# Attention probabilities weighted for two key tiles per visit of TensorE, with four buffers instead of two

## The chip, the core and the metric

The kernel runs on one core of one Trainium2 chip. The metric is the device time of one execution in microseconds; a kernel's time is the median of several.

## The reference

x has two rows of 1024 tokens with 128 channels, in float32. Four layers are added to it one after the other: a gated recurrence with an MLP, a mixture of low-rank experts, an attention, and the experts again. The change is in the attention:

```python
attn = jax.nn.softmax(jnp.einsum('bhqd,bhkd->bhqk', q, k) * scale, axis=-1)
...
attn = attn + rel_bias
out = jnp.einsum('bhqk,bhkd->bhqd', attn, v)
```

There are 16 heads of 8 channels, so per row and head a matrix of 1024 x 1024 scores, its softmax, and the values weighted with it.

## The kernel before

The kernel is written engine by engine: each has its own program, and they meet at counting semaphores. No scheduler changes the order; what stands in a program is done in that order, and a wait holds up all that is behind it on its engine.

The attention works on 8 groups, each four heads of one row of the input. A group has 16 **steps**: two halves of 512 queries (q) times eight tiles of 128 keys (t). In step s:

- TensorE makes four **scores** (`scores`, L1402), one head each: 128 keys x 512 queries into one of three PSUM banks. A score waits until the third exponential before it is done.
- ScalarE takes the exponential of each (`step`, L731) into a buffer of probabilities, `probs[s % 2]`. Before a step it waits (`pv_done`) until the weighing that read this buffer is done.
- TensorE **weighs** the values with the probabilities of the step before (`weigh`, L1416): four float32 matmuls of 128 keys x 32 columns, one per head, each on its own 32 columns of the array, all added up in the bank `pv_bank` over eight steps. The profile records each as two passes, so a weighing is 8 records. Once per half, ScalarE copies the bank out (`take_pv`, L721).

Beside the scores of one group TensorE and VectorE work on the **ring**: 36 items per group that go through two slots of two PSUM banks each. 32 items are products for the maxima of the next groups (`max_item`, L1339, two matmuls of 512 columns), which VectorE reduces (L1028). The others are the turn of the 32 maxima (L1345, which VectorE splits in three parts, L1033 to L1039), the bias product (L1353), its turn (L1359) and the turn of the output (L1366). An item is filled when the item two before it has been emptied (`ring_emptied`). `beside` deals the items to the steps: two for each, three for every fourth. In a step TensorE does, in this order: score 0, item, score 1, score 2, weighing, item, score 3, and a third item if there is one.

A round begins at step 2 (`FIRST`) of a group and ends with step 1 of the next. Six rounds run in a loop of two passes over three rounds; then comes the round that prepares the last group, with no items for a group after it, and the last group's own steps, among which the first pieces of the last expert layer stand. The weighing of a group's last step is made in step 0 of the next group, or after the steps for the last group.

```python
RING = NEXT_MAXES[:4] + [("bias", 0, 0), NEXT_MAXES[4], ("bias_turn", 0, 0)] + NEXT_MAXES[5:] + AFTER_NEXT + [("out", 0, 0)]
...
    return banks[:, 2 * (n % 2):2 * (n % 2) + 2, :]
...
    share = RING[j * len(RING) // STEPS:(j + 1) * len(RING) // STEPS]
```

## Time and profile before

| what | value |
|---|---|
| median of 3 runs | 742.9 us (740.99 to 742.91) |
| the profiled execution, from first to last instruction | 738.4 us |
| TensorE busy (matmul) | 666.5 us, 90% |
| VectorE busy | 533.7 us, 72% |
| ScalarE busy | 381.2 us, 52% |
| mean granted clock of TensorE | 0.961 |

The span is that of one profiled execution; for it no time is recorded apart from the span, and the runs' median lies 4.5 us above it. A busy time is the time in which at least one instruction of the engine ran. Where engines hand work to each other all the time, the share alone does not say which of them sets the pace; that is read from what each waits for. The attention's steps lie between 256 and 664 us.

### The profile page before, as it was taken

The page shows a single profiled execution, that of the slowest core. Times are in us where ns is not written, and L with a number is a line of the kernel's source. Part 1 is how long each engine was busy: PE and PEld are TensorE (multiplying, and loading weights), DVE is VectorE, ACT ScalarE, POOL GpSimd, SP SyncE. Part 2 cuts the span into 40 slices and gives each one's busy share as a digit, 9 for nine tenths or more (in the row PEclk, how much of TensorE's full clock was granted, in tenths as well). Part 3 has the DMA queues.
Part 4 walks back from the last instruction along what each step waited for, and adds up shares of the span by engine and source line. Part 5 has one row for each costly group of instructions (what it writes and reads, how often), then busy time and mean ns, then how long its engine had stood idle before and what let it go on. Part 6 is the DMA issues. An engine that isn't in the chain of part 4 may idle for free.

```text
span 738.4 us, 10515 instructions
## 1 busy us (share of the span) xinstructions
PE 666.5 (90%) x3192; PEld 254.5 (34%) x3192; DVE 533.7 (72%) x956; ACT 381.2 (52%) x687; POOL 104.9 (14%) x100
## 2 busy tenths in 40 slices
PE   3988898999777699999999899999999998988997
PEld 1434344444343222332322232332322322324443
DVE  5379788746699868868878768868788688308744
ACT  2745133333203057767767657766667677882231
POOL 5910110001044411020020020020100202002000
PEclk9998899999969789999999999999999999999999
DMA  8000000000313102012012020030120000000000
GB/s 253 5 1 0 1 0 1 1 0 0 112 67 122 58 28 95 2 41 83 4 56 66 17 83 28 18 99 9 32 91 3 2 0 2 2 1 0 1 28 28
DMA packets 21413, 26.59 MB, mean 36 GB/s; under 512 B 3312, under 2 KB 12016, under 8 KB 21360
## 3 DMA queue, kind: packets, MB, share of 16 engines
q1 hardware_dynamic: 20496, 25.39, 10.8%
q8 instruction: 29, 0.48, 0.3%
q0 software_dynamic: 144, 0.52, 0.2%
q14 instruction: 24, 0.20, 0.1%
q10 hardware_dynamic: 720, 0.00, 0.1%
HBM read 21.52 MB, written 4.19 MB: 35 GB/s over the span
## 4 chain that ended last, share of the span: by engine, by line
PE 69%; DVE 19%; ACT 4%; issue 2%; DMA 2%; DVEq 1%; POOL 1%; SPq 1%; POOLq 0%; ACTq 0%
PE banks L1416 17%; PE banks L1339 15%; PE banks L1402 14%; PE banks L1154 6%; DVE negmax L1028 6%; PE banks L1224 4%; PE banks L1265 3%; PE banks L1353 2%; PE banks L1215 2%; PE banks L1161 2%; DVE arena L886 1%; ACT arena L731 1%; DVE arena L936 1%; DVE stats L783 1%; PE banks L1366 1%
## 5 line engine op out<-in xcount | busy, mean ns | idle before, releaser
L1028 DVE TENSOR_REDUCE negmax<-banks 128x1 f32<-128x1024 f32 x256 | 300.8, 1217 | 68.6 <-PE banks L1339 67.4
L731 ACT ACTIVATE arena<-banks 128x512 f32<-128x512 f32 x512 | 271.7, 601 | 144.1 <-PE banks L1402 140.6
L1339 PE MATMUL banks<-arena 72*128 72x512 bf16 x512 | 161.3, 400 | 23.6 <-DVE negmax L1028 19.7
L1402 PE MATMUL banks<-arena 75*128 75x512 bf16 x512 | 160.2, 384 | 6.7 <-ACT arena L731 3.1
L1416 PE MATMUL banks<-arena 128*32 128x512 f32 x1024 | 138.1, 612 | 0.7 <-ACT arena L731 0.7
L1339 PEld LDWEIGHTS banks<-arena 72*128 72x128 bf16 x512 | 37.8, 100 | 163.0 <-DVE negmax L1028 77.0
L1402 PEld LDWEIGHTS banks<-arena 75*128 75x128 bf16 x512 | 48.6, 98 | 95.7 <-ACT arena L731 48.0
L495 POOL TENSOR_TENSOR rstd<-veps,neghalf 128x4 f32<-128x4 f32 (+1 forms) x24 | 27.1, 1129 | 247.3 <-DVE veps L802 192.1
L1224 PE MATMUL banks<-arena,bT 128*128 128x512 f32 x128 | 60.1, 593 | 1.6 <-ACT arena L585 1.6
L585 ACT ACTIVATE arena<-banks 128x512 f32<-128x512 f32 (+1 forms) x56 | 32.2, 595 | 53.1 <-PE banks L1154 22.7
L886 DVE TENSOR_SCALAR arena<-banks,bi 128x512 f32<-128x512 f32 x32 | 23.8, 745 | 34.7 <-PE banks L1224 34.7
L562 POOL TENSOR_TENSOR pause<-neghalf 128x8 f32<-128x8 f32 x7 | 1.4, 199 | 309.9 <-PE banks L1353 309.9
L1224 PEld LDWEIGHTS banks<-arena,bT 128*128 128x128 f32 x128 | 24.2, 190 | 32.2 <-issue 29.9
L1416 PEld LDWEIGHTS banks<-arena 128*32 128x32 f32 x1024 | 20.3, 108 | 39.3 <-issue 33.2
L1215 PE MATMUL banks<-hT,wiT 128*128 128x512 f32 x64 | 32.9, 615 | 0.0
L1161 PE MATMUL banks<-ident,nt 128*128 128x128 f32 x80 | 13.7, 313 | 20.4 <-DVE nt L812 11.9
L546 POOL TENSOR_TENSOR arena<-arena,t_last 128x2048 f32<-128x2048 f32 x8 | 28.8, 3599 | 0.0
L585 ACT ACTIVATE hT<-banks 128x512 f32<-128x512 f32 x12 | 6.8, 596 | 31.8 <-PE banks L1161 31.8
L1265 PE MATMUL banks<-arena,woT 128*128 128x512 f32 x48 | 22.1, 597 | 0.3
L585 ACT ACTIVATE x<-banks,bi 128x512 f32<-128x512 f32 x16 | 11.0, 687 | 20.3 <-PE banks L1224 20.3
L783 DVE BATCH_NORM_STATS2 stats<-x 128x6 f32<-128x128 f32 x80 | 17.4, 280 | 5.4 <-DMA x<-in_x 4.5
L585 ACT ACTIVATE oT<-banks,bo 128x512 f32<-128x512 f32 x8 | 5.5, 687 | 30.4 <-PE banks L1265 30.4
(128 smaller groups left out, 614.1 us busy)
## 6 DMA issues: line engine op xcount, KB each, us to landing
arena<-qk_scratch SPq DMA_DIRECT2D x192, 48.0 KB
arena<-in_tab SPq DMA_DIRECT2D x8, 1024.0 KB, 6.8
qk_scratch<-arena SPq DMA_DIRECT2D x8, 384.0 KB, 2.8
out<-x SPq DMA_DIRECT2D x4, 256.0 KB, 2.3
x<-in_x SPq DMA_DIRECT2D x1, 512.0 KB, 4.5
x<-in_x POOLq DMA_DIRECT2D x1, 512.0 KB, 7.7
arena<-nm_part SPq DMA_DIRECT2D x24, 8.0 KB, 1.9
w_aT<-in_w_aT SPq DMA_DIRECT2D x1, 256.0 KB, 6.5
```

Source lines behind the costliest of these rows:

```text
L546: pool.tensor_tensor(varying, bias_raw[:, :, ::-1], t_last[:, bass.ds(G * GH, GH)].unsqueeze(2).broadcast_to([P, GH, BIASW]), ALU.subtract ...
L585: act.activation(dst, banks[:, BANK[name], :], func, **kw).then_inc(signal or act_emptied, 1)
L731: act.activation(probs[s % 2][:, h, :], score_bank(g, n), ACT.Exp, scale=SCALE).then_inc(exp_done, 1)
L886: dve.tensor_scalar(h1[:, c % 2, :], bank(name), bi[:, c:c + 1], 0.0, ALU.add, ALU.max).then_inc(dve_emptied, 1)
L1028: return dve.tensor_reduce(negmax[:, buf, k:k + 1], slot.rearrange("p a b -> p (a b)"), axis=AXX, op=ALU.max, negate=True)
L1154: last = pe.matmul(banks[:, BANK[name], :], lhsT, rhs, start=i == 0, stop=i == len(terms) - 1)
L1215: pe.matmul(banks[:, BANK[name], :], chunk(wiT, c), half(hT[:, b], h), start=True, stop=False, skip_group_check=True)
L1224: pe.matmul(banks[:, BANK[name], :], chunk(bT, c), half(moe[b][4][:, k, :], h), start=False, stop=k == 1, skip_group_check=True).then_inc( ...
L1265: last = pe.matmul(banks[:, BANK[name], :], woT[:, c, :], moe[b][2][h][:, c, :], start=c == 0, stop=c == FC - 1)
L1339: last = pe.matmul(slot[:, half_, :], qs[0:STACK, buf, h, t * P:(t + 1) * P], ks[0:STACK, buf, h, half_ * HALF:(half_ + 1) * HALF], start= ...
L1402: pe.matmul(score_bank(g, n), ks[0:DEPTH, g % BUFS, h, t * P:(t + 1) * P], qs[0:DEPTH, g % BUFS, h, q * HALF:(q + 1) * HALF], start=True, ...
L1416: last = pe.matmul(pv_bank[32 * h:32 * h + VW, :], vpg[:, g % BUFS, t, h, :], probs[s % 2][:, h, :], start=t == 0, stop=t == NT - 1)
```

## The change

`probs` gets two more buffers, in tiles that lie idle during the attention (x0 and oT, each 128 x 2048 float32 by the view taken of it). ScalarE writes step s into `probs[s % 4]`. TensorE no longer weighs in every step: in an even step s it weighs the steps s-2 and s-1 one right after the other, in the place where the single weighing stood, and in an odd step not at all. Step 0 of a group takes the last two of the group before. ScalarE copies the weighed bank out in step 1 and step 9, behind the first exponential, where before it did so in step 0 and step 8, behind the third. Its waits on `pv_done` follow.

```diff
--- before.py
+++ after.py
@@ -314,6 +314,8 @@
         qk_part = [m.bitcast(BF16).rearrange("p (w n t) -> p w n t", w=2, n=NPART) for m in (words_0, words_1)]
 
         probs = [m.rearrange("p w t -> p (w t)").rearrange("p (h t) -> p h t", h=GH) for m in qk_rest]
+
+        probs += [m[:].rearrange(f"p {axes} -> p ({axes})").rearrange("p (h t) -> p h t", h=GH) for m, axes in ((x0, "b t c"), (oT, "b t"))]
         varying = words_1[:, 0:GH * BIASW].rearrange("p (h c) -> p h c", h=GH)
         qs = q_words.bitcast(BF16).rearrange("p (n h t) -> p n h t", n=BUFS, h=GH)
 
@@ -722,16 +724,16 @@
 
             def step(G, g, s):
 
-                if s >= 2 or not (isinstance(G, int) and G == 0):
-
-                    act.wait_ge(pv_done, at(G, pv_done, s - 1))
+                if s >= len(probs) or (s < FIRST and not (isinstance(G, int) and G == 0)):
+
+                    act.wait_ge(pv_done, at(G, pv_done, 0 if s == 1 else s - len(probs) + 1))
                 for h in range(GH):
                     n = s * GH + h
                     act.wait_ge(scores_filled, at(G, scores_filled, n + 1))
-                    act.activation(probs[s % 2][:, h, :], score_bank(g, n), ACT.Exp, scale=SCALE).then_inc(exp_done, 1)
-                    if h == GH - 2 and s == 0 and not (isinstance(G, int) and G == 0):
+                    act.activation(probs[s % len(probs)][:, h, :], score_bank(g, n), ACT.Exp, scale=SCALE).then_inc(exp_done, 1)
+                    if h == 0 and s == 1 and not (isinstance(G, int) and G == 0):
                         take_pv(G - 1, 1)
-                    if h == GH - 2 and s == NT:
+                    if h == 0 and s == NT + 1:
 
                         act.wait_ge(ring_filled, at(G, ring_filled, 0))
                         take_pv(G, 0)
@@ -1413,9 +1415,18 @@
 
                         pe.wait_ge(pv_out, at(G, pv_out, q))
                 for h in range(GH):
-                    last = pe.matmul(pv_bank[32 * h:32 * h + VW, :], vpg[:, g % BUFS, t, h, :], probs[s % 2][:, h, :],
+                    last = pe.matmul(pv_bank[32 * h:32 * h + VW, :], vpg[:, g % BUFS, t, h, :], probs[s % len(probs)][:, h, :],
                                      start=t == 0, stop=t == NT - 1)
                 last.then_inc(pv_done, 1)
+
+            def weigh_two(G, g, s):
+
+                if s:
+                    weigh(G, g, s - 2)
+                    weigh(G, g, s - 1)
+                elif not (isinstance(G, int) and G == 0):
+                    weigh(G - 1, g - 1, STEPS - 2)
+                    weigh(G - 1, g - 1, STEPS - 1)
 
             def step(G, g, s, fill_item, ring):
 
@@ -1424,10 +1435,8 @@
                     fill_item(ring[0])
                 scores(G, g, s, 1)
                 scores(G, g, s, 2)
-                if s:
-                    weigh(G, g, s - 1)
-                elif not (isinstance(G, int) and G == 0):
-                    weigh(G - 1, g - 1, STEPS - 1)
+                if s % 2 == 0:
+                    weigh_two(G, g, s)
                 if len(ring) > 1:
                     fill_item(ring[1])
                 scores(G, g, s, 3)
@@ -1501,7 +1510,7 @@
                     logits(1, 0)
                 if s == X_STEP:
                     turn_products(1, 0)
-            weigh(G, G, STEPS - 1)
+            weigh_two(G + 1, G + 1, 0)
             for c in range(FC):
                 base(1, 0, c)
                 if c == 0:
```

On TensorE, here are two steps of the straight part behind the loop, in the round that prepares the last group (steps 6 and 7 of a group, with two items each), from one weighing to the next but one. L1416 is the weighing, L1402 a score, L1339 the product for a maximum. Before:

```order
L1416 MATMUL banks<-arena 32x512 x4
L1339 MATMUL banks<-arena 128x512 x2
L1402 MATMUL banks<-arena 128x512 x2
L1339 MATMUL banks<-arena 128x512 x2
L1402 MATMUL banks<-arena 128x512 x2
L1416 MATMUL banks<-arena 32x512 x4
L1339 MATMUL banks<-arena 128x512 x2
L1402 MATMUL banks<-arena 128x512 x2
L1339 MATMUL banks<-arena 128x512 x2
L1402 MATMUL banks<-arena 128x512 x2
L1416 MATMUL banks<-arena 32x512 x4
```

In the changed kernel the same stretch reads (L1418 is the weighing, L1404 the score, L1341 the product; x and oT are the new buffers):

```order
L1418 MATMUL banks<-arena 32x512 x8
L1341 MATMUL banks<-arena 128x512 x2
L1404 MATMUL banks<-arena 128x512 x2
L1341 MATMUL banks<-arena 128x512 x2
L1404 MATMUL banks<-arena 128x512 x2
L1341 MATMUL banks<-arena 128x512 x2
L1404 MATMUL banks<-arena 128x512 x2
L1341 MATMUL banks<-arena 128x512 x2
L1404 MATMUL banks<-arena 128x512 x2
L1418 MATMUL banks<-x,arena 32x512 x4
L1418 MATMUL banks<-oT,arena 32x512 x4
```

Between two visits there are now four products and eight scores in a row, and each visit has eight matmuls instead of four.

The second place is on TensorE too, in the same round behind the last product for a maximum, where steps have no items left; L1345 is the turn of the maxima. Before:

```order
L1345 MATMUL banks<-ident,negmax 32x128
L1402 MATMUL banks<-arena 128x512 x2
L1416 MATMUL banks<-arena 32x512 x4
L1402 MATMUL banks<-arena 128x512 x4
L1416 MATMUL banks<-arena 32x512 x4
L1402 MATMUL banks<-arena 128x512 x4
L1416 MATMUL banks<-arena 32x512 x4
```

And in the changed kernel:

```order
L1347 MATMUL banks<-ident,negmax 32x128
L1404 MATMUL banks<-arena 128x512 x6
L1418 MATMUL banks<-arena 32x512 x8
L1404 MATMUL banks<-arena 128x512 x8
L1418 MATMUL banks<-x,arena 32x512 x4
L1418 MATMUL banks<-oT,arena 32x512 x4
```

Here eight scores stand between two visits, where four stood before.

## Rows read from the trace of the kernel before

**Rows 1.** Groups of instructions in one round, 323.2 to 373.9 us

```profile
L1028 DVE TENSOR_REDUCE negmax<-banks 128x1 f32<-128x1024 f32 x33 | 38.8, 1217 | 8.3 <-PE banks L1339 8.2 <-issue 0.2
L731 ACT ACTIVATE arena<-banks 128x512 f32<-128x512 f32 x65 | 34.6, 601 | 16.2 <-PE banks L1402 15.7
...
L1339 PE MATMUL banks<-arena 72*128 72x512 bf16 x64 | 19.3, 382 | 0.9 <-DVE negmax L1028 0.9
L1416 PE MATMUL banks<-arena 128*32 128x512 f32 x128 | 17.1, 605 | 0.0
```


**Rows 2.** The chain that ended last (start us, us, what)

```profile
272.51 2.29 PE banks L1353 x32
...
323.24 2.29 PE banks L1353 x32
...
350.86 0.99 PE banks L1416 x8
...
356.68 0.99 PE banks L1416 x8
```


**Rows 3.** Timeline (start us, us, engine, line, what), three steps

```profile
328.84 1.06 PE L1416 MATMUL banks<-arena 128*32 128x512 f32 x8
...
330.48 3.48 DVE L1028 TENSOR_REDUCE negmax<-banks 128x1 f32<-128x1024 f32 x3 [1.42 <-PE banks L1339]
...
331.76 0.60 PE L1339 MATMUL banks<-arena 72*128 72x512 bf16 x2 [0.45 <-DVE negmax L1028]
...
332.20 0.60 PE L1402 MATMUL banks<-arena 75*128 75x512 bf16 x2
...
332.73 1.07 PE L1416 MATMUL banks<-arena 128*32 128x512 f32 x8
...
333.73 0.61 PE L1339 MATMUL banks<-arena 72*128 72x512 bf16 x2
...
334.37 2.36 DVE L1028 TENSOR_REDUCE negmax<-banks 128x1 f32<-128x1024 f32 x2 [0.41 <-PE banks L1339]
...
335.56 1.06 PE L1416 MATMUL banks<-arena 128*32 128x512 f32 x8
```


**Rows 4.** Timeline, TensorE's weight loads at a bias product

```profile
323.16 0.16 PEld L1353 LDWEIGHTS banks<-arena 128*32 128x32 f32 x8 [0.42 <-issue]
...
323.62 0.13 PEld L1353 LDWEIGHTS banks<-arena 128*32 128x32 f32 x4 [0.30 <-issue]
324.05 0.13 PEld L1353 LDWEIGHTS banks<-arena 128*32 128x32 f32 x4 [0.30 <-issue]
```


**Rows 5.** Timeline, a step without products

```profile
614.30 1.06 PE L1416 MATMUL banks<-arena 128*32 128x512 f32 x8
...
615.30 0.82 PE L1402 MATMUL banks<-arena 75*128 75x512 bf16 x3
...
615.73 2.06 ACT L731 ACTIVATE arena<-banks 128x512 f32<-128x512 f32 x4 [0.33 <-PE banks L1402]
...
616.38 0.39 PE L1402 MATMUL banks<-arena 75*128 75x512 bf16 x1 [0.26 <-ACT arena L731]
...
616.70 1.07 PE L1416 MATMUL banks<-arena 128*32 128x512 f32 x8
```


**Rows 6.** Timeline, VectorE around the split of the maxima

```profile
354.94 0.28 DVE L1033 CAST nm_part<-banks 32x128 bf16<-32x128 f32 x1 [0.16 <-PE banks L1345]
...
355.30 0.28 DVE L1035 TENSOR_TENSOR nm_rest<-banks,nm_part 32x128 f32<-32x128 f32 x1
...
356.17 3.47 DVE L1028 TENSOR_REDUCE negmax<-banks 128x1 f32<-128x1024 f32 x3
```


**Rows 7.** Windows (from:to, us, busy us and count per engine, granted clock)

```profile
418.00:422.00 4.00, 1.71 (x11) 0.86 (x9) 2.20 (x6) 0.99 (x3) 0.00 (x0) 1.00 0.12 33
422.00:430.00 8.00, 8.00 (x45) 2.09 (x48) 4.59 (x4) 4.22 (x8) 0.00 (x0) 0.79 0.18 59
640.00:664.00 24.00, 21.03 (x124) 5.32 (x124) 5.11 (x19) 20.42 (x42) 0.00 (x0) 1.00 0.00 1
```


## The prediction

> **What bounds the kernel now.** I began with the page's part on costly groups, narrowed to one round of the attention [rows 1]. A round is one group of four heads: 50.73 us from one bias product to the next [rows 2]. In it VectorE spends 38.8 us in 33 maxima and is idle 8.3 us before them, waiting for TensorE's products; ScalarE spends 34.6 us in exponentials and is idle 16.2 us, again only for TensorE (L1402). No row has ScalarE waiting for a weighing, which is what a buffer of probabilities comes free with. So the two further buffers by themselves buy nothing; what counts is the order on TensorE.
>
> Then the timeline, step by step [rows 3]. A plain step (four scores, two products for maxima, one weighing) goes from the weighing at 332.73 to that at 335.56: 2.83 us. Matmuls of 512 columns follow each other at 0.217 us, a product for a maximum (two of them) takes 0.435, and the weighing takes 1.00 from its start to the next matmul. The two scores ahead of it start at 332.20 and would be through at 332.64, so 0.09 us more go in before it. Sum: 4 x 0.217 + 2 x 0.435 + 1.09 = 2.83. TensorE paces this step. One step in four has a third product and takes 3.89 us (328.84 to 332.73), where its own work is 3.26: the rest it stands still ahead of the product at 331.76 (idle 0.45 in the row), until VectorE's first reduce has released a slot.
>
> That gives VectorE's three constants, all from [rows 3]. Its reduce starts 0.64 us after the product's first matmul (333.73 to 334.37). Reduces follow each other at 1.13 us (three in 3.48, the last 1.22 long). TensorE enters the slot again 1.28 us after the reduce's start (330.48 to 331.76). There are two slots. Check: from the end of a weighing the next product is at 0, its reduce at 0.64, its slot free at 1.92; then one product, two scores, the entry and the weighing, 0.435 + 0.434 + 0.09 + 1.00 = 1.96: 3.88, against 3.89 measured.
>
> **The change, part by part.** The visits go from one per step to one of two weighings in every even step; 128 visits (eight groups of 16 steps) become 64, with the same matmuls in all.
>
> *What a merged visit saves.* The bias product is the same kind of matmul, four groups in a row without a switch [rows 4]. Its first group starts at 323.16, the second pass at 323.62, the next group at 324.05. So a group of 512 columns takes 0.88 us when another follows, and the 0.12 on top in a single visit is paid on leaving. A double visit is then D = 0.88 + 1.00 = 1.88 us, with the same 0.09 ahead. Against two singles (2.18) it saves 0.21 us; 64 of them, if TensorE paced everything, 13.4 us. The Trainium skill, page TensorEngine Tiling (Array Packing), "Key Properties", says that changing the tiling mode drains TensorE. The trace agrees (0.09 and 0.12 us), and by that rule alone the change is right. The same page, "PSUM Bottleneck", warns that emptying PSUM may become the bound.
>
> *What it costs.* TensorE now feeds VectorE nothing for 1.88 us at a time, and VectorE can hold at most two filled slots. I walk one pair (light step, then the heavy step with the visit) from the end of a visit:
> - product A starts at 0, its reduce at 0.64, its slot is free at 1.92
> - product B, the light step's first, is filled well before VectorE comes to it; its reduce is at 0.64 + 1.13 = 1.77, its slot free at 1.77 + 1.28 = 3.05
> - product C, the light step's second, goes into A's slot at 1.92; its reduce is at 2.90
> - product D, the heavy step's first, needs B's slot. With nothing to wait for TensorE would be there at 2.61 (six scores and three products); it starts at 3.05, and two scores, the visit and everything behind are queued after it
> - 0.435 + 0.434 + 0.09 = 0.96 later the visit starts, at 4.01, and ends at 5.89.
>
> Two plain steps took 5.67: **+0.22**. With a third product in the light step one more reduce lies in the way: 5.89 + 1.13 = 7.02, against 3.89 + 2.83 = 6.72: **+0.30**. D's reduce starts at 2.90 + 1.13 = 4.03 and is over at 5.25, so VectorE idles from there to 5.89 + 0.64, 1.3 us a pair; that is where the saved switches go. ScalarE does not matter here: a pair's eight exponentials take some 3.9 us at 0.49 each [rows 5].
>
> *The pairs of one round* (eight):
> - three plain pairs: 3 x 0.22 = 0.66
> - two with a third product: 2 x 0.30 = 0.60
> - the pair with the turn of the maxima. Its split holds VectorE for 1.23 us (354.94 to 356.17) and gives its slot back at 355.58 [rows 6]. The turn's slot is free at 1.92; the split runs behind product B's reduce, from 2.90 to 4.13. C now waits for B's slot (3.05), D starts at 3.70 (the turn's slot is free at 3.54), the visit at 4.66, its end is 6.54. Today the two steps take 356.68 - 350.86 = 5.82 [rows 2]: +0.72. Dear, because today the step's wait hides the split
> - the pair with the bias product (2.29 us, TensorE's own) starts it at 3.05 rather than at once and comes to +0.1. The one after it, whose turn of the bias costs VectorE 0.28, to -0.1: zero together.
>
> Sum 1.98 us a round. Six full rounds: 11.9. The seventh has its products up to the turn: +0.7. Its last steps and the last group run without products.
>
> *Steps without products.* Today one takes 2.40 us (614.30 to 616.70), set by ScalarE: with three score banks the step's third score comes 0.65 after the previous step's last exponential starts (615.73 to 616.38), the visit 0.32 behind it, its end 1.00 later, and the fourth score's exponential 0.43 after that (615.30 to 615.73) [rows 5]. With a double visit: 0.65 + 0.32 + 1.88 + 0.43 = 3.28 to that exponential, and four more at 0.49 (four in 2.06, the last 0.6 long) until the light step's last: 5.24, against 4.80: +0.4. Of ten such pairs about five are bare (+2.0); three hold transposes or logits, which fill the wait (about +0.5 together); at the end the last exponentials and one joint visit replace two (about -0.5). I take +2.0.
>
> Total 11.9 + 0.7 + 2.0 = +14.6 us: span 738.4 to 753.0. The median 742.9 lies 4.5 above the profiled span, and I leave that as it is: **757.5 us**.
>
> The take-over of the weighed bank by ScalarE moves one step later, behind a score that exists anyway. The next visit is over 5 us off, so I cost it at nothing; uncovered it is 0.6 us (one activation), 16 times. That ScalarE passes over no visit wait is in [rows 1]. The new wait for weighings ahead of a step's exponentials asks for a visit that TensorE makes before it issues that step's scores.
>
> **Bounds.** The least D is four passes at 0.43 with nothing for switching, 1.72 [rows 4]: 0.16 less in 63 pairs, 747. Product waits that come 0.1 later each (semaphores, register updates) in the 53 pairs with products: 762.
>
> **Rivals.**
> 1. *Faster: TensorE paces all the pairs.* Then 13.4 us go: 729.5. For it: today TensorE's matmul groups show almost no idle before them (0.9 us at L1339 [rows 1]). Against it: the pair's length by VectorE's chain is 4.01 + D, so it turns only at D under 1.66, less than four passes. Or the release at 1.28 would have to fall by over 0.2. Chance 0.07.
> 2. *Same: the losses come only where a third product or the turn stands* (2 x 0.30 + 0.72 a round), and the other five pairs gain 0.21 each: +0.3 a round, +2, and as much back from the pairs at the end: about 743. Chance 0.05.
> 3. *Slower still: the clock falls.* At 418 to 422 TensorE is busy 1.71 of 4.00 us and the granted clock in the next 8 us is 0.79, part at 1.2 GHz instead of 2.4 [rows 7]: 0.21 x 8 = 1.7 us. One such dip a round more: 757.5 + 13 = 771. Against it: from 640 to 664 TensorE is busy 21.0 of 24 us, in gaps like those I expect, and the clock stays 1.00. The Trainium skill, page TensorE: Matmul & The Clock Gate, "A second HAM failure mode: psum-queue depth-cycling", tells of short idle times between matmul groups that make the clock swing; no row here shows that. Chance 0.05.
>
> The forecast (starved VectorE, 747 to 764) has 0.83. That the change would not do what it says I leave out: the order of the built program shows the double visits.
>
> **Numbers.** A measurement here can tell 0.3%, 2.2 us. Range 747 to 766: the bounds, with a little above for smaller clock losses; 0.07 + 0.05 + part of 0.05 and some of the spread lie outside. Faster 0.07 (rival 1), same 0.04, slower 0.89 (rival 2 mostly counts as same).
>
> **What the trace after would show.** Double visits of 1.88 us in 16 records; visits of even steps 5.9 and 7.0 us apart; the heavy step's first product waiting for a reduce; VectorE idle some 1.3 us before the reduce behind each visit; a round of 52.7 us; pairs without products 5.2 us apart. I am wrong if the visits come 5.4 us apart and VectorE's idle time there is under 1 us (rival 1), if D is not 1.88, or if the clock column shows new dips.

## The result: 3.9% slower, more than forecast

| | before | changed |
|---|---|---|
| median | 741.94 us (740.50 to 742.91) | 769.60 us (764.44 to 772.35) |
| ratio of the times, 95% interval | | 1.039 [1.034, 1.044] |
| span of the profiled execution | 738.4 us | 762.7 us |

Forecast were 757.5 us and a range up to 766. The side was right, the size was not. Medians here are over all executions of a kernel, while ratios leave out executions over 1.5% above that kernel's fastest, so a ratio can differ from the quotient of the medians beside it.

From the page of the changed kernel: the engines' busy times, VectorE's maxima and TensorE's products for them (busy us, mean ns of one, idle us before them and what ended it):

```profile
span 762.7 us, 10501 instructions
...
PE 677.1 (89%) x3192; PEld 262.1 (34%) x3192; DVE 531.3 (70%) x956; ACT 375.4 (49%) x687; POOL 105.2 (14%) x100
...
L1030 DVE TENSOR_REDUCE negmax<-banks 128x1 f32<-128x1024 f32 x256 | 298.3, 1217 | 88.3 <-PE banks L1341 86.9
L1341 PE MATMUL banks<-arena 72*128 72x512 bf16 x512 | 162.7, 403 | 30.8 <-DVE negmax L1030 24.8
```

The same two lines of the kernel before:

```profile
L1028 DVE TENSOR_REDUCE negmax<-banks 128x1 f32<-128x1024 f32 x256 | 300.8, 1217 | 68.6 <-PE banks L1339 67.4
...
L1339 PE MATMUL banks<-arena 72*128 72x512 bf16 x512 | 161.3, 400 | 23.6 <-DVE negmax L1028 19.7
```

VectorE does the same 256 maxima, but waits 86.9 us for products instead of 67.4, and TensorE waits 24.8 us for VectorE instead of 19.7. Both waits grew, as two engines do that hand work to each other through too few slots; the walk below shows that it is so. A pair of steps without a third product, in the timeline (start us, us, engine, line, what):

```profile
345.51 1.93 PE L1418 MATMUL banks<-arena 128*32 128x512 f32 x16
...
347.37 0.60 PE L1341 MATMUL banks<-arena 72*128 72x512 bf16 x2
...
348.01 4.62 DVE L1030 TENSOR_REDUCE negmax<-banks 128x1 f32<-128x1024 f32 x4 [1.27 <-PE banks L1341]
...
348.24 0.59 PE L1341 MATMUL banks<-arena 72*128 72x512 bf16 x2
...
349.29 0.60 PE L1341 MATMUL banks<-arena 72*128 72x512 bf16 x2
...
350.42 0.60 PE L1341 MATMUL banks<-arena 72*128 72x512 bf16 x2
...
350.86 0.60 PE L1404 MATMUL banks<-arena 75*128 75x512 bf16 x2
...
351.39 1.06 PE L1418 MATMUL banks<-x,arena 128*32 128x512 f32 x8
```

Read it against [rows 3]. The visit is one run of 16 records, and the next product starts 1.86 us after it (345.51 to 347.37; forecast 1.88). VectorE has waited 1.27 us (forecast 1.3) and reduces four slots in a row. The heavy step's first product stands at 350.42, 3.05 behind the first product, to the hundredth as the walk had it; only then come two scores and the next visit. From visit to visit: 351.39 - 345.51 = 5.88 us, forecast 5.89. The pair with the turn of the maxima, from its first product on:

```profile
353.25 0.60 PE L1341 MATMUL banks<-arena 72*128 72x512 bf16 x2
...
355.17 0.28 PE L1347 MATMUL banks<-ident,negmax 128*32 128x128 f32 x1
...
356.16 0.27 DVE L1035 CAST nm_part<-banks 32x128 bf16<-32x128 f32 x1
...
356.30 0.61 PE L1341 MATMUL banks<-arena 72*128 72x512 bf16 x2 [0.63 <-DVE negmax L1030]
...
356.96 0.59 PE L1341 MATMUL banks<-arena 72*128 72x512 bf16 x2
...
357.92 1.93 PE L1418 MATMUL banks<-arena 128*32 128x512 f32 x16
```

Product C waits for B's slot (idle 0.63 in its row) and starts 3.05 us behind the first product (353.25 to 356.30), as forecast. The visit comes 357.92 - 351.39 = 6.53 us after the one before (forecast 6.54). Pairs with a third product take 7.01 and 7.09 (forecast 7.02).

Where the 24.3 us of span went. The cuts are the starts of the first score, of the bias products (as in [rows 2]) and of the last pass of the last weighing:

| stretch | before | changed | difference | forecast |
|---|---|---|---|---|
| start to first score | 256.2 | 252.9 | -3.3 | 0 |
| to the first bias product | 16.3 | 17.5 | +1.2 | 0 |
| five rounds | 50.73 each | 52.69 each | +9.8 | +9.9 |
| the round across the loop's jump | 54.59 | 58.45 | +3.9 | +2.0 |
| 7th bias product to 8th | 43.2 | 47.4 | +4.2 | +2.7 with the next |
| 8th bias product to the last weighing's last pass | 39.4 | 47.9 | +8.5 | |
| the rest | 75.0 | 75.05 | 0 | 0 |

So the rounds came out as computed, +1.96 against +1.98. The excess stands at the end, where steps have no products, and in the round across the jump (there TensorE's clock is at half for 6.8 us instead of 3.4). Windows of the changed kernel's end (from:to, us, busy us and count of PE, PEld, DVE, ACT, POOL, granted clock, two DMA columns):

```profile
640.00:650.00 10.00, 9.61 (x81) 3.23 (x74) 1.28 (x4) 5.89 (x12) 0.00 (x0) 1.00 0.00 0
660.10:663.50 3.40, 3.40 (x17) 0.60 (x16) 1.88 (x6) 1.17 (x3) 0.00 (x0) 0.50 0.00 0
666.90:670.30 3.40, 3.37 (x15) 0.69 (x17) 0.00 (x0) 1.71 (x4) 0.00 (x0) 0.50 0.00 0
680.50:684.00 3.50, 3.50 (x17) 0.59 (x16) 0.00 (x0) 1.21 (x3) 0.00 (x0) 0.51 0.02 5
```

Three stretches at 0.50, that is 1.2 GHz instead of 2.4, and a fourth at 625.9; the ten us from 640 are at full clock. The kernel before had none from 425.4 us to its end. A fifth, at 704.4, lies behind the attention, where the time did not change (75.05 us against 75.02). The other new thing is a wait that I had costed at nothing:

```profile
636.65 0.60 ACT L723 ACTIVATE arena<-banks 128x512 f32<-128x512 f32 x1
...
637.40 1.06 PE L1368 MATMUL banks<-ident,arena 128*128 128x128 f32 x8 [1.54 <-ACT arena L723]
```

The turn of the output stands 1.54 us still until ScalarE has taken the weighed bank over.

### The profile page after: what moved, and what is told of

It is laid out like the page before. It is cut to its first block, busy times and chain, and to the rows that moved or that the text cites. A ratio compares the mean times of both kernels' runs of the same rounds, so it can differ in the third digit from the quotient of the medians.

```text
span 762.7 us, 10501 instructions
## 1 busy us (share of the span) xinstructions
PE 677.1 (89%) x3192; PEld 262.1 (34%) x3192; DVE 531.3 (70%) x956; ACT 375.4 (49%) x687; POOL 105.2 (14%) x100
## 4 chain that ended last, share of the span: by engine, by line
PE 54%; DVE 26%; issue 9%; ACT 5%; DVEq 2%; DMA 2%; POOL 1%; SPq 1%; POOLq 0%; ACTq 0%
PE banks L1418 17%; DVE negmax L1030 14%; PE banks L1341 10%; PE banks L1404 6%; PE banks L1156 6%; PE banks L1226 4%; PE banks L1355 2%; PE banks L1267 2%; PE banks L1217 2%; PE banks L1163 2%; DVE arena L888 1%; ACT oT L733 1%; DVE arena L938 1%; PE banks L1368 1%; DVE stats L785 1%
## 5 line engine op out<-in xcount | busy, mean ns | idle before, releaser
L1030 DVE TENSOR_REDUCE negmax<-banks 128x1 f32<-128x1024 f32 x256 | 298.3, 1217 | 88.3 <-PE banks L1341 86.9
L1341 PE MATMUL banks<-arena 72*128 72x512 bf16 x512 | 162.7, 403 | 30.8 <-DVE negmax L1030 24.8
L733 ACT ACTIVATE arena<-banks 128x512 f32<-128x512 f32 x256 | 138.7, 612 | 94.5 <-PE banks L1404 94.3
L1404 PE MATMUL banks<-arena 75*128 75x512 bf16 x512 | 164.1, 389 | 10.0 <-issue 2.7
L733 ACT ACTIVATE x<-banks 128x512 f32<-128x512 f32 x128 | 72.7, 600 | 84.9 <-PE banks L1404 84.0
L1341 PEld LDWEIGHTS banks<-arena 72*128 72x128 bf16 x512 | 37.3, 100 | 147.1 <-DVE negmax L1030 110.0
L1404 PEld LDWEIGHTS banks<-arena 75*128 75x128 bf16 x512 | 49.2, 98 | 98.7 <-ACT arena L733 19.3
L1418 PE MATMUL banks<-arena 128*32 128x512 f32 x512 | 69.0, 661 | 0.0
L733 ACT ACTIVATE oT<-banks 128x512 f32<-128x512 f32 x128 | 66.0, 612 | 0.0
L1418 PE MATMUL banks<-x,arena 128*32 128x512 f32 x256 | 35.0, 619 | 0.0
L1418 PE MATMUL banks<-oT,arena 128*32 128x512 f32 x256 | 34.1, 605 | 0.1
L1418 PEld LDWEIGHTS banks<-arena 128*32 128x32 f32 x512 | 14.3, 117 | 36.9 <-issue 29.5
```

Source lines behind the costliest of these rows:

```text
L733: act.activation(probs[s % len(probs)][:, h, :], score_bank(g, n), ACT.Exp, scale=SCALE).then_inc(exp_done, 1)
L1030: return dve.tensor_reduce(negmax[:, buf, k:k + 1], slot.rearrange("p a b -> p (a b)"), axis=AXX, op=ALU.max, negate=True)
L1341: last = pe.matmul(slot[:, half_, :], qs[0:STACK, buf, h, t * P:(t + 1) * P], ks[0:STACK, buf, h, half_ * HALF:(half_ + 1) * HALF], start= ...
L1404: pe.matmul(score_bank(g, n), ks[0:DEPTH, g % BUFS, h, t * P:(t + 1) * P], qs[0:DEPTH, g % BUFS, h, q * HALF:(q + 1) * HALF], start=True, ...
L1418: last = pe.matmul(pv_bank[32 * h:32 * h + VW, :], vpg[:, g % BUFS, t, h, :], probs[s % len(probs)][:, h, :], start=t == 0, stop=t == NT - 1)
```

## Experiments

The theory after the result had three parts: (V) in the rounds VectorE's two slots set the pair, as forecast; (E) at the end the double visit holds ScalarE's chain up, and the later take-over holds the turn of the output up; (C) the longer waits of TensorE lower its clock more often. Rivals: the four buffers themselves cost something; the take-over is the cause; the clock alone is.

**Buffers alone.** The kernel before with the four buffers and their waits, one weighing a step.

```diff
+        probs += [m[:].rearrange(f"p {axes} -> p ({axes})").rearrange("p (h t) -> p h t", h=GH) for m, axes in ((x0, "b t c"), (oT, "b t"))]
...
+                    act.wait_ge(pv_done, at(G, pv_done, 0 if s == 1 else s - len(probs) + 1))
...
+                    act.activation(probs[s % len(probs)][:, h, :], score_bank(g, n), ACT.Exp, scale=SCALE).then_inc(exp_done, 1)
```

> The kernel before with four buffers of probabilities and still one weighing per step. Theory (what costs time is the order on TensorE, not the buffers): same time as before, 741.9 us within 2, rounds of 50.7 us. Rival (the buffers in x0 and oT cost something, or the later release helps): more than 745 or less than 740 us.

740.04 us against 739.93; 0.999 [0.996, 1.003]; a round 50.71 us. Within 0.4%, the buffers neither cost nor bring anything. The loss comes with the order on TensorE and the later take-over, a loss of clock that they bring included.

**Singles at the end, doubles in the rounds.**

```diff
@@ -1437,3 +1437,6 @@
                 scores(G, g, s, 2)
-                if s % 2 == 0:
+                last = isinstance(G, int) and (G == GROUPS - 1 or (G == GROUPS - 2 and s > 12))
+                if last:
+                    weigh(G if s else G - 1, g if s else g - 1, (s - 1) % STEPS)
+                elif s % 2 == 0:
                     weigh_two(G, g, s)
@@ -1512,3 +1515,3 @@
                     turn_products(1, 0)
-            weigh_two(G + 1, G + 1, 0)
+            weigh(G, G, STEPS - 1)
             for c in range(FC):
```

> The changed kernel, but from step 13 of the seventh group on one weighing per step again. Theory (about half of the loss sits in the steps without products: ScalarE starved, a new wait for the take-over, clock dips that these gaps bring): rounds stay at 52.7 us, the stretch from the seventh bias product to the last weighing falls from 95.3 us to some 83.5, no dips there, 752 to 756 us in all. Rival (the dips come by chance or from the rounds): the clock dips stay and the time is above 762 us.

760.85 us, 1.027 [1.022, 1.033]. The rounds stay at 52.69. The stretch from the seventh bias product to the last weighing takes 46.0 + 39.9 = 85.9 us against 95.3, and no part of it is at half clock. The same windows of both kernels, the changed one first:

```profile
600.00:650.00 50.00, 44.59 (x266) 13.38 (x265) 34.40 (x87) 32.00 (x62) 4.12 (x4) 0.97 0.00 1
650.00:688.00 38.00, 33.38 (x172) 10.14 (x170) 7.13 (x29) 25.46 (x52) 0.00 (x0) 0.87 0.00 1
```

```profile
600.00:650.00 50.00, 45.49 (x284) 13.64 (x282) 36.43 (x90) 33.64 (x65) 7.41 (x5) 1.00 0.01 1
650.00:688.00 38.00, 34.34 (x200) 11.97 (x200) 9.29 (x37) 28.94 (x58) 0.00 (x0) 1.00 0.00 1
```

With single visits TensorE is busy 45.49 and 34.34 us there instead of 44.59 and 33.38, and the clock is 1.00 in both. The time came out over the 752 to 756 expected. The end is 2.4 us longer than the 83.5 expected. In the profile the edit takes 9.4 us off the end, but the first score comes at 257.4 us instead of 252.9, in code that the edit does not touch, so the spans differ by 4.7 only (758.0 and 762.7). Over all profiled executions with whole reduces, of the kernel before and of the changed ones, the first score comes at 250.9 to 258.1 us; single spans compare kernels no closer than that. Parts E and C share the end; this edit does not separate them.

**Doubles at the end, singles in the rounds.**

```diff
@@ -1437,3 +1437,7 @@
                 scores(G, g, s, 2)
-                if s % 2 == 0:
+                last = isinstance(G, int) and (G == GROUPS - 1 or (G == GROUPS - 2 and s > 14))
+                if not last:
+                    if s or not (isinstance(G, int) and G == 0):
+                        weigh(G if s else G - 1, g if s else g - 1, (s - 1) % STEPS)
+                elif s % 2 == 0:
                     weigh_two(G, g, s)
```

> The reverse: one weighing per step up to step 14 of the seventh group, pairs only behind it. Theory: rounds of 50.7 us as before, the stretch from the seventh bias product to the last weighing at 93 to 95 us with clock dips, 752 to 757 us in all. Rival (the end costs what I predicted, 2 us): 744 us.

The six executions lie far apart: their median is 762.13 us, and the ratio, 1.021 [1.013, 1.029], rests on three of them (751.51, 753.54 and 761.18 us). The profiled one took 764.73, with some 91 us at half clock against 74 in the changed kernel's. In it the end is 46.6 + 46.5 us, as expected, with half-clock stretches at 633, 667 and 681. The rounds are 52.02, not the 50.7 expected:

```profile
346.35 1.06 PE L1418 MATMUL banks<-oT,arena 128*32 128x512 f32 x8
...
349.18 0.60 ACT L723 ACTIVATE arena<-banks 128x512 f32<-128x512 f32 x1
...
349.84 1.07 PE L1418 MATMUL banks<-arena 128*32 128x512 f32 x8 [0.58 <-ACT arena L723]
```

With take-overs in steps 1 and 9 a single visit waits for the bank twice a round, 3.49 us from visit to visit instead of 2.83, which makes up the 1.29 us. So the later take-over costs nothing only where visits are a pair apart. Some 8 us of this kernel's loss are of that kind and not the end's, so its time says less about the end than was meant.

**The take-over where it was.**

```diff
@@ -733,5 +733,5 @@
                     act.activation(probs[s % len(probs)][:, h, :], score_bank(g, n), ACT.Exp, scale=SCALE).then_inc(exp_done, 1)
-                    if h == 0 and s == 1 and not (isinstance(G, int) and G == 0):
+                    if h == GH - 2 and s == 0 and not (isinstance(G, int) and G == 0):
                         take_pv(G - 1, 1)
-                    if h == 0 and s == NT + 1:
+                    if h == GH - 2 and s == NT:
```

> The changed kernel with ScalarE's copy of the weighed bank back in steps 0 and 8, behind the third exponential, as before the change. Theory (the later copy only matters where no products stand between it and the turn of the output, once, in the last round): rounds 0.1 us shorter, the wait of 1.5 us ahead of the last round's turn of the output gone, 1 to 3 us faster than the changed kernel. Rival (the later copy hides ScalarE's wait for the visit in every round): rounds longer by 0.3 us or more each, slower by 2 us or more.

766.72 us, 1.032 [1.026, 1.038] over four of six executions; rounds 52.69 as in the changed kernel, 7th to 8th bias product 46.07 instead of 47.37: the 1.3 us of the wait at the turn of the output. The rest of the end takes 44.5 us instead of 47.9, with one half-clock stretch instead of three. In the total that is within the spread: the changed kernel beside it has 1.038 [1.034, 1.043].

**The heavy step's first product behind its third score.**

```diff
@@ -1433,3 +1433,3 @@
                 scores(G, g, s, 0)
-                if len(ring) > 0:
+                if len(ring) > 0 and s % 2:
                     fill_item(ring[0])
@@ -1437,2 +1437,4 @@
                 scores(G, g, s, 2)
+                if len(ring) > 0 and s % 2 == 0:
+                    fill_item(ring[0])
                 if s % 2 == 0:
```

> The changed kernel, in which an even step makes its first product behind the third score, right before the double visit, so that VectorE has more left to do when TensorE turns away. Theory (VectorE starved through two slots sets the pair): plain pairs 5.63 instead of 5.88 us, those with a third product 6.59 instead of 7.01, rounds of some 50.4 us; the end as in the changed kernel; 750 to 757 us. Rival (TensorE's own work or the weighing sets the pair): rounds stay at 52.7 us and the time at 765 to 770.

764.65 us, 1.034 [1.029, 1.039]; a round 52.48, expected 50.4: a miss. Third-product pairs came down to 6.58 as expected, but plain pairs went up to 6.08:

```profile
348.74 0.10 PEld L1404 LDWEIGHTS banks<-arena 75*128 75x128 bf16 x1 [0.40 <-ACT oT L733]
...
348.97 0.60 PE L1341 MATMUL banks<-arena 72*128 72x512 bf16 x2
...
349.50 1.07 PE L1418 MATMUL banks<-x,arena 128*32 128x512 f32 x8
349.61 1.23 DVE L1030 TENSOR_REDUCE negmax<-banks 128x1 f32<-128x1024 f32 x1 [0.20 <-PE banks L1341]
```

The wait is now at a score: its weight load (the first row) stands 0.40 us until ScalarE (L733) is done. With three score banks the heavy step's third score can go 3.47 us after the visit's end. From there 0.22 + 0.435 (the product now behind it) + 0.09 + 1.88 make 6.09 us. VectorE waits a mere 0.20. So a second chain, ScalarE's, lies just under VectorE's: without the product in it, 3.47 + 0.22 + 0.09 + 1.88 = 5.66 us a pair.

**VectorE made faster, in both kernels.** Before, and the same edit on the changed kernel:

```diff
@@ -730,3 +730,3 @@
                     act.wait_ge(scores_filled, at(G, scores_filled, n + 1))
-                    act.activation(probs[s % 2][:, h, :], score_bank(g, n), ACT.Exp, scale=SCALE).then_inc(exp_done, 1)
+                    act.activation(probs[s % 2][:, h, :], score_bank(g, n), ACT.Exp, scale=SCALE / 8).then_inc(exp_done, 1)
                     if h == GH - 2 and s == 0 and not (isinstance(G, int) and G == 0):
@@ -1027,3 +1027,3 @@
             def max_item(slot, buf, k):
-                return dve.tensor_reduce(negmax[:, buf, k:k + 1], slot.rearrange("p a b -> p (a b)"), axis=AXX, op=ALU.max, negate=True)
+                return dve.tensor_reduce(negmax[:, buf, k:k + 1], slot[:, 0, :], axis=AXX, op=ALU.max, negate=True)
```

> The kernel before with reduces over 512 of the 1024 columns (maxima over half the keys, and a smaller exponent so that nothing overflows; the computation is changed), so that VectorE is out of the way. Every theory: plain steps stay at 2.83 us, steps with a third product lose VectorE's wait, 3.26 instead of 3.89; rounds of some 48.3 us.

716.8 us in one execution; rounds 49.38, plain steps 2.83 as they were, third-product steps 3.36 instead of 3.89. The round was expected at 48.3: the third-product steps kept 0.10 us over 3.26, the step with the turn of the output came down to 3.71 only, and the one with the bias product (4.79) not at all.

> The same two edits in the changed kernel (maxima over half the keys, a smaller exponent). Theory of two chains (VectorE's through the two slots gives 5.88 us a plain pair, and behind it ScalarE's through the three score banks gives 3.47 + 0.22 + 0.09 + 1.88 = 5.66): plain pairs 5.66, pairs with a third product 5.88, so that even with a fast VectorE merging gives nothing on a plain pair. Rival (VectorE alone eats the gain): plain pairs at TensorE's own 5.45.

725.8 us in one execution; rounds 48.72. Plain pairs, visits in the timeline:

```profile
331.80 1.92 PE L1418 MATMUL banks<-arena 128*32 128x512 f32 x16
...
337.45 1.06 PE L1418 MATMUL banks<-x,arena 128*32 128x512 f32 x8
```

5.65 us, where ScalarE's chain gives 5.66. Third-product pairs 6.14 (expected 5.88). The rounds of the changed kernel are now the shorter by 0.66 us, where with whole reduces they are the longer by 1.96: that bears V out, VectorE's slots turn the merging's gain in the rounds into a loss. The total is still 9 us longer than its counterpart's, all of it outside these rounds: the end takes 7.1 us more, the round across the jump 3.6, the start 1.6, and the five rounds 3.3 less.

**ScalarE made faster as well.**

```diff
@@ -732,3 +732,3 @@
                     act.wait_ge(scores_filled, at(G, scores_filled, n + 1))
-                    act.activation(probs[s % len(probs)][:, h, :], score_bank(g, n), ACT.Exp, scale=SCALE).then_inc(exp_done, 1)
+                    act.activation(probs[s % len(probs)][:, h, 0:HALF // 2], score_bank(g, n)[:, 0:HALF // 2], ACT.Exp, scale=SCALE / 8).then_inc(exp_done, 1)
                     if h == 0 and s == 1 and not (isinstance(G, int) and G == 0):
@@ -1029,3 +1029,3 @@
             def max_item(slot, buf, k):
-                return dve.tensor_reduce(negmax[:, buf, k:k + 1], slot.rearrange("p a b -> p (a b)"), axis=AXX, op=ALU.max, negate=True)
+                return dve.tensor_reduce(negmax[:, buf, k:k + 1], slot[:, 0, :], axis=AXX, op=ALU.max, negate=True)
```

> The changed kernel with reduces over half the columns and exponentials over 256 of the 512 queries (the other half of the probabilities is left as it was, and the exponent is smaller; the computation is changed): VectorE and ScalarE are both out of the way. Theory: plain pairs at TensorE's own 8 x 0.217 + 4 x 0.435 + 0.09 + 1.88 = 5.45 us, with a third product 5.88. Rival (a merged visit costs TensorE something that I don't see): 5.6 or more.

711.8 us in one execution; rounds 47.6. The visits:

```profile
332.87 1.92 PE L1418 MATMUL banks<-arena 128*32 128x512 f32 x16
...
338.30 1.07 PE L1418 MATMUL banks<-x,arena 128*32 128x512 f32 x8
```

5.43 us. TensorE's own work is 8 x 0.217 + 4 x 0.435 + 0.09 + 1.88 = 5.45: only now does it pace the pair. The three bounds of a plain pair in the changed order are 5.88 (VectorE's slots), 5.66 (score banks), 5.45 (TensorE).

**Three repairs together**: singles at the end, the take-over as it was, the heavy step's product behind the third score.

> Three edits in the changed kernel together: one weighing per step from step 13 of the seventh group on, the even step's first product behind the third score, and the copy of the weighed bank in steps 0 and 8. Theory: the sum of the single effects: rounds of 52.3 us, the end within 3 us of the kernel before, 2 to 2.6% slower than before. Rival (together they free the gain of the merged visits): within 0.5% of the kernel before.

754.32 us, 1.019 [1.014, 1.024]; rounds 52.48. The end takes 83.2 us, against 82.7 in the kernel before. It is the best version with double visits, and still slower than before.

**The waits at the end filled** with scores computed twice (same operands, same bank), so that TensorE is not idle.

```diff
@@ -1403,4 +1403,7 @@
                 t, q = s % NT, s // NT
-                pe.matmul(score_bank(g, n), ks[0:DEPTH, g % BUFS, h, t * P:(t + 1) * P], qs[0:DEPTH, g % BUFS, h, q * HALF:(q + 1) * HALF],
-                          start=True, stop=True).then_inc(scores_filled, 1)
+                idle = isinstance(G, int) and (G == GROUPS - 1 or (G == GROUPS - 2 and s > 13)) and h in ((2, 3) if s % 2 else (0, 1))
+                for _ in range(1 + idle):
+                    last = pe.matmul(score_bank(g, n), ks[0:DEPTH, g % BUFS, h, t * P:(t + 1) * P], qs[0:DEPTH, g % BUFS, h, q * HALF:(q + 1) * HALF],
+                                     start=True, stop=True)
+                last.then_inc(scores_filled, 1)
```

> The changed kernel; in the steps without products, where TensorE stands and waits for ScalarE, each score that follows such a wait is computed twice into its bank (the second result is the same), so that TensorE is busy instead of idle. It is more work for nothing. Theory (the gaps let the granted clock fall, and that costs some 8 us at the end): no dips between the turn of the last maxima and the last weighing, the stretch from the seventh bias product to the last weighing at 87 to 89 us instead of 95.3, and the kernel 5 to 8 us faster than the changed one. Rival (the dips come by chance, or cost nothing): dips stay, the same time as the changed kernel or up to 2 us slower.

767.14 us, 1.037 [1.032, 1.042], beside the changed kernel again:

> The changed kernel once more, beside the next three on the same chip. Every theory: 3.4 to 4.4% over the kernel before, rounds of 52.7 us.

769.27 us, 1.038 [1.034, 1.043]. In the profiles the end of the filled kernel takes 91.8 us with one half-clock stretch, that of the changed kernel beside it 97.1 with five. But 87 to 89 us with none were expected, and a kernel 5 to 8 us faster; the medians differ by 2.1 us and the intervals overlap.

**Waits filled in the rounds too.** Two duplicates at a heavy step's first score and one at a light step's third, in place of that condition:

```diff
+                    if late:
+                        idle = h in ((2, 3) if s % 2 else (0, 1))
+                    else:
+                        idle = (h == 2) if s % 2 else 2 * (h == 0)
```

> The changed kernel; scores are computed twice (the second result is the same), and where TensorE stands waiting longest three times, in the rounds too, so that it has hardly an idle moment. Theory (its gaps in the rounds and at the end let the granted clock fall, which costs some 10 us in most executions): mean granted clock 0.953 or more instead of 0.944, rounds no longer than 53.2 us, 3 us or more faster than the changed kernel. Rival (the clock falls for another reason): clock at 0.94 to 0.95, the same time or slower.

774.13 us, 1.047 [1.041, 1.053]. The mean clock is 0.957, where the changed kernel's 16 executions have 0.946 (other chips, so this is the weaker comparison), but rounds were 54.47 us (expected 53.2 at most): plain pairs take 6.08 instead of 5.88, since the duplicates push the heavy step's first product back. With one duplicate in place of two:

```diff
+                        idle = (h == 2) if s % 2 else (h == 0)
```

> Like the kernel with scores computed twice everywhere, but never three times, which there made each pair 0.2 us longer (the first product of the even step then came at 3.26 instead of 3.05 us). Now the repeats fit into the waits. Theory (the gaps cost clock, and the clock costs time): plain pairs at 5.88 as in the changed kernel, mean granted clock 0.953 or more, 5 us or more faster than the changed kernel on this chip. Rival (what raised the clock there were the longer rounds, or the clock's falls cost nothing here): clock below 0.950, or the time within 3 us of the changed kernel.

> The changed kernel beside the next two on the same chip: 3.4 to 4.4% over the kernel before, mean granted clock near 0.944.

765.74 us, 1.035 [1.031, 1.039], beside 766.43, 1.036 [1.031, 1.040] for the changed kernel. The clock part held, mean 0.956 against 0.948. Windows in the rounds, of the changed kernel in this third profile, then of the filled one:

```profile
343.00:346.80 3.80, 3.17 (x14) 0.97 (x13) 3.80 (x4) 3.62 (x7) 0.00 (x0) 1.00 0.32 125
346.80:350.20 3.40, 3.40 (x16) 0.77 (x18) 1.90 (x2) 1.11 (x3) 0.00 (x0) 0.50 0.02 5
350.20:360.00 9.80, 9.04 (x51) 2.71 (x44) 7.14 (x7) 6.43 (x13) 0.00 (x0) 1.00 0.00 1
...
568.70:572.10 3.40, 3.40 (x17) 0.54 (x16) 1.18 (x2) 0.92 (x2) 0.00 (x0) 0.50 0.00 0
```

```profile
346.80:350.20 3.40, 3.40 (x24) 1.01 (x22) 2.14 (x2) 1.66 (x4) 0.00 (x0) 1.00 0.00 0
500.00:560.00 60.00, 58.43 (x359) 19.62 (x356) 45.05 (x47) 38.59 (x74) 4.09 (x3) 1.00 0.19 57
```

At 346.8 and 568.7 the changed kernel is at 0.50, and each such stretch makes its round 54.3 to 54.4 instead of 52.69, +1.6 to +1.7; the filled kernel, busy 58.43 of 60 us, keeps 1.00. But its rounds are 53.23: plain pairs still take 5.88, and the pairs with the turn of the maxima and of the output 0.2 us more each, where duplicates delay products. The gain of 5 us expected was not there. The longer rounds account for some 3 us of it; that the clock gave as much is not shown by itself.

**The idea turned on the kernel before**: in steps 2, 6, 10 and 14, behind which a third product is waited for, the first product goes behind the third score.

```diff
@@ -1422,3 +1422,4 @@
                 scores(G, g, s, 0)
-                if len(ring) > 0:
+                late = s % 4 == 2
+                if len(ring) > 0 and not late:
                     fill_item(ring[0])
@@ -1426,2 +1427,4 @@
                 scores(G, g, s, 2)
+                if len(ring) > 0 and late:
+                    fill_item(ring[0])
                 if s:
```

> The kernel before (one weighing per step), where in the step after one with a third product the first product comes behind the third score instead of behind the first. The same chain of constants says: it may start at 1.92 us behind the weighing, TensorE does three scores meanwhile, the pair's first step takes 3.45 instead of 3.89 us, rounds 1.3 to 1.7 us shorter, 730 us or 1.1 to 1.5% faster than before, clock no lower. Rival (another chain, ScalarE's, takes over as it did in the changed kernel): rounds within 0.3 us of 50.73 and the same time.

735.58 us against 739.23; **0.995 [0.991, 0.999]** over ten of twelve executions. Over all, the means are 736.6 (12) and 739.8 (17), 0.4% apart. So it is probably a little faster than the kernel before, near the limit of what a comparison tells here, and not by the 1.1 to 1.5% expected. The timeline of one such step:

```profile
330.71 5.82 DVE L1028 TENSOR_REDUCE negmax<-banks 128x1 f32<-128x1024 f32 x5 [1.42 <-PE banks L1339]
...
331.17 0.81 PE L1402 MATMUL banks<-arena 75*128 75x512 bf16 x3
...
332.00 0.61 PE L1339 MATMUL banks<-arena 72*128 72x512 bf16 x2
...
332.53 1.07 PE L1416 MATMUL banks<-arena 128*32 128x512 f32 x8
...
333.53 0.61 PE L1339 MATMUL banks<-arena 72*128 72x512 bf16 x2
```

Three scores run where TensorE stood still in [rows 3], and the step takes 3.46 us instead of 3.89 (forecast 3.45). A round is 49.86, -0.87; -1.3 to -1.7 were expected. Two of the steps give 0.43 each. Around the turn of the output two steps take 3.71 + 3.02 us, where they took 3.89 + 2.84, so nothing is gained there. The clock was to be no lower, but its executions spend a mean of 64 us at half clock against 58: by the 0.35 us for each us found below, an estimate, that takes 2 of the 5 us that six rounds save.

## Why the prediction was wrong in size

**What held.** D = 1.88 (1.86 from the double visit to the next product); pairs of 5.89, 7.02 and 6.54, measured 5.88, 7.01 to 7.09 and 6.53; VectorE idle 1.3; rounds +1.98 (+1.96). Rival 1 (TensorE paces all) needed pairs of 5.45; shown false by the changed kernel's 5.88 and, from the other side, by the two kernels with faster VectorE and ScalarE, which reach 5.65 and 5.43. Rival 2 (only third products and turn cost) fails with the plain pairs' +0.22. Buffers at nothing: shown, within 0.4%. The Trainium skill's rule on mode switches (TensorEngine Tiling (Array Packing), "Key Properties") would alone speak for the change. The trace agrees with the rule, and it was beside the point: the 0.21 us a visit is saved and comes out as VectorE's wait.

**The step that failed first: "Steps without products", "I take +2.0", with the +0.7 of the seventh group.** Measured +12.7 over the two stretches. Part of that is order and part is clock, which the three profiles of the changed kernel tell apart: with three, four and five half-clock stretches of 3.4 us in them these two stretches take 94.2, 95.3 and 97.1 us, about 1.4 us a stretch, which leaves some 7 of the 12.7 us with none. The same comes out pair by pair, where each pair that was at half clock is taken from a profile in which it was not (another one of the changed kernel, for two of them the one with the early take-over):

| part of the end | forecast | measured without half clock |
|---|---|---|
| the seventh group's products and last turn | +0.7 | +0.96 |
| five pairs with scores and weighings, or little more | +2.0 | +2.36 |
| the pair with the turn of the output and the bias product | +0.5 with the next two | +1.46 |
| the pair with the first transposes and the logits | | +0.57 |
| the pair with the later transposes | | +1.07 |
| last exponentials and joint visit | -0.5 | +0.42 |
| sum | +2.7 | +6.84 |

Bare pairs are as computed, 5.21 to 5.26 us (5.24). Wrong was "three hold transposes or logits, which fill the wait": these three cost 3.1 us more, not 0.5. In one of them it is mostly the take-over, costed "at nothing": "The next visit is over 5 us off" looked at the next visit, not at the turn of the output, which reads the copy and waits 1.54 us. Wrong was also that the joint visit at the end saves 0.5 us. The other 5.8 us are clock, 1.0 to 1.8 for each of the four stretches. In the prediction's sum that had no term.

**The second: rival 3, the clock, priced as an alternative with 0.05.** It holds in addition to the forecast. That its 771 lies near the 769.6 measured is luck: it had one more fall in every round and nothing at the end. "From 640 to 664 TensorE is busy 21.0 of 24 us ... and the clock stays 1.00" was read as evidence that the expected gaps do no harm; the changed kernel falls to 0.50 in that very place. Neither the busy share nor the longest wait tells the two apart there: the kernel before is busy 5.80 of 7.00 us from 657 to 664, with a wait of 0.69, and keeps its clock, while the changed one is busy 3.44 of 4.10 us from 656.0 to 660.1, with no wait over 0.26, and falls. Over the executions with a recorded clock the kernel before spent a mean of 59 us at half clock (56 beside the experiments, from each one's mean clock and span), the changed one 83 (16 executions, 72 to 94 us); within a kernel, each us more at half clock goes with 0.35 us more span (before) or 0.32 (changed). So, as an estimate, 24 x 0.35, about 8 us, of a mean difference of 28 are clock, and 20 are order. That filling the waits raises the clock is shown by the kernel that fills the rounds with single duplicates (0.956 against 0.948 on the same chip), and the one with more of them points the same way (0.957); that it brings net time is not shown, since there the duplicates delayed the products.

**The third: the 4.5 us between median and span.** Each execution here has a time 1.7 to 1.9 us over its span (764.44 and 762.7). The rest of the distance belonged to other executions, presumably to their clock, and was no constant to add. It did not make the forecast too low: with 1.8 instead of 4.5 it would have been 754.8.

Put together: a line through each kernel's executions puts their spans at 60 us of half clock at 759 and 738.8 us, 20 apart, where 14.6 were forecast, and some 8 come on top by clock. For the changed kernel 60 us lies below all that its executions had, so this is an extrapolation.

**Overlooked: the chain of the score banks** (5.66), which lies 0.22 under VectorE's. "ScalarE does not matter here" compared its busy time with the pair, not its banks' return. It changed no term, but made the product's move fail.

**Open.** The changed kernel's executions fall to half clock in different places: at the end in all three profiles, but three, four and five times, and within the rounds in two of them; what decides where was not found. What in the merged order brings the falls, if not the share or the length of the waits, is open too. In the ledger, the first stretch's -3.3 lies in code that the change doesn't touch; the second's +1.2 holds the first double visits, partly at half clock in both kernels, and was not taken apart.

## What to carry to other kernels

Work that is merged on a producing engine is also a longer silence for its consumers: before merging, walk one period with the number of slots between them, and compare silence plus refill with what the slots hold; here that walk was right to 0.01 us for the plain pairs and to 0.07 for the others. Do the same walk for each stretch with another mix of work, and for each reader of a step that is moved, instead of one estimate for all. Where an engine waits for a slot, work that needs none may go ahead of it: that brought about 0.5% where merging lost 3.9%.

## What the hardware showed

- In the third profile of the changed kernel TensorE fell to half clock behind a stretch in which it was busy 3.17 of 3.80 us, and no wait in its rows there is over 0.31 us. The kernel before, with a wait of 0.45 in every fourth step [rows 3], kept full clock from 425.4 us to its end. The same pattern stands in every round of the changed kernel, and most rounds kept full clock. The Trainium skill, page TensorE: Matmul & The Clock Gate, "A second HAM failure mode: psum-queue depth-cycling", tells of short idle times between matmul groups with which the clock goes down and up again and again; the runs fit it, with a mean of 83 us at half clock against 59, but don't show that the idle times themselves are the cause.
- Over whole executions the loss from half clock is less than half of the time spent in it (0.35 us for each us in the kernel before, 0.32 in the changed one). A stretch of 3.4 us costs 1.6 to 1.7 us in a round of the changed kernel, 1.0 to 1.8 at the end, and nothing visible at 704.4, presumably because TensorE's work there would have waited for other engines anyway; this was not tried by itself.
- A visit to the 32-column tiles costs 0.09 us on entering and 0.10 to 0.12 on leaving, whether it has 4 matmuls or 8: the next product starts 1.00 us after a single visit's start and 1.86 after a double one's (345.51 to 347.37), of which 0.88 for each four matmuls.
